# Graph attention with residual and layer norm: the row scale found at a slot's end, its sums in PSUM, the moments one slot later

## The chip, the cores and the metric

One NeuronCore of a Trainium2 chip (trn2). The metric is the device time of one launch in microseconds; the kernel before took 638.26 us (median of 3 runs, 637.56 to 639.02).

## What is computed

64 graphs of 128 nodes and 384 channels, 12 heads of 32 channels, in float32. The adjacency matrix is both spatial and edge encoding, so it enters the scores twice. A row of scores that is all zero gives zero attention.

```python
q = (x @ Wq.T); k = (x @ Wk.T); v = (x @ Wv.T + bv)          # split in 12 heads of 32
scores = einsum('bqhd,bkhd->bhqk', q, k) * 384**-0.5 + (adj + adj)[:, None]
row_nonzero = any(scores != 0, axis=-1)
p = softmax(where(row_nonzero, scores, -inf)); p = nan_to_num(p)
y = x + einsum('bhqk,bkhd->bqhd', p, v).reshape(b, n, h) @ Wo.T + bo
out = (y - mean(y)) / sqrt(var(y) + 1e-5)
```

## The kernel before

Everything is in one hand-ordered program: each engine has its own loop over slots, with semaphores between them. Slot b (b from -1 to 64) works on several graphs at once: it begins graph b+1 and ends graph b-1. Matmuls with weights are done in three terms from a high and a low part (`TERMS`), so each is 9 matmuls for 384 channels.

TensorE, slot b: `turn(b)` (48 transposes of the probabilities), `score(b+1)` (12 heads into the four banks `scores_ps`, three column blocks m of 128 each), one and a half tiles of the next group's queries or keys (`project`), `values(b+1)`, `project_out(b-1)` into `scores_ps[0]`, `attend(b)` into `scores_ps[1]`. Slots 59 and later have no `project`. `score` waits for the bias passes, `y_ready` and `att_done` of earlier slots, since those read the banks.

VectorE, slot b, in this order: `normalise(b-1)` (writes `att_n`, L626), `find_scale(b)` (L589 to L615), `bias_and_max(b+1, 0)` and `(b+1, 1)` (L558: per head adds the adjacency, multiplies by -2, and takes the row's minimum as `neg_max`; the queries carry half the scale), `attention_low(b-1)` (L630), `bias_and_max(b+1, 2)`, `keep_turned_high(b)`, `keep_first(b)`, `keep_v(b+1)`, `residual(b-1)` (y, L639, then `bn_stats` L642 and `bn_aggr` L644).

ScalarE (ACT), slot b: `attention_high(b-1)` (L503), `keep_turned_low(b)`, `softmax_top(b+1, m)` (L473: 12 exponentials with row sums, one `probs_ready` a column block), `keep_second(b)`, `normalised(b-2)` (writes `out_n`), `split_x_high`.

GpSimd (POOL), slot b: `find_rstd(b-2)` (L295 to L303: rstd and shift from the moments), `sum_scores(b+1)` (L287: halves the rows of `nscores` by additions into `tree`, in parts of `PARTS` and in `TREE` levels; a row's sum together with `neg_max` tells whether the row is all zero), `add_bias(b)` (L275), `split_x_low` (L268; in three slots of four).

`find_scale` makes of the tree's rest a sum (`total`), of that and `neg_max` a flag (`nonzero`), of the row sums a reciprocal (`recip`), and of both the row scale, transposed. The scale goes through memory (SP's DMAs to `scale_mem` and back to `scale_t`) so that it lies along the columns of the attention output, where `normalise` multiplies with it. The last graph takes the direct way: `scale_n` goes through TensorE's transposes.

Of the kernel before, what the change touches and what calls it, by code (L numbers as in the profile page):

```python
# [10 lines left out]
P = 128  # L11
NB = 64
HID = 384
HEADS = 12
D = HID // HEADS
KT = HID // P
HPT = P // D
# [8 lines left out]

TERMS = ((HI, HI), (HI, LO), (LO, HI))
FULL = KT * len(TERMS)
TREE = 3
REST = P >> TREE  # L30

PARTS = ((0, 2 * HPT), (2 * HPT, HEADS))
STEPS = TREE * len(PARTS)
XBUFS = 3

# [3 lines left out]
def build(nc, xt, xn, adj, wq, wk, wv, wo, bv, bo, out):  # L39
    with ExitStack() as ctx:  # L40
        def sb(name, shape, dt=F32):
            return ctx.enter_context(nc.sbuf_tensor(name, shape, dt))

        def ps(name, shape):
            return ctx.enter_context(nc.psum_tensor(name, shape, F32))

        def sem(name):
            return ctx.enter_context(nc.semaphore(name))
# [21 lines left out]
        neg_max = sb("neg_max", [P, 2, HEADS])  # L70
        row_sum = sb("row_sum", [P, 2, HEADS])
        tree = sb("tree", [P, 2, HEADS, P // 2])
        total = sb("total", [P, HEADS])
        nonzero = sb("nonzero", [P, HEADS])
        recip = sb("recip", [P, HEADS])
        row_scale = sb("row_scale", [P, D])
        scale_rows = sb("scale_rows", [P, 2, D])
# [19 lines left out]
        scores_ps = [ps(f"scores_ps{j}", [P, 512]) for j in range(HPT)]  # L97
# [3 lines left out]

        turn_ps = [qk_ps[0], v_ps, qk_ps[1], spare_ps]
        att_ps = scores_ps[1]


        scale_mem = nc.dram_tensor("scale_mem", (2, D, P), F32, kind="Internal").ap()
# [34 lines left out]
        total_done = sem("total_done")  # L141
        recip_done = sem("recip_done")
        nonzero_done = sem("nonzero_done")
        scale_found = sem("scale_found")
# [18 lines left out]
        def has(b):  # L163
            return 0 <= b < NB

        def wait(eng, semaphore, value):

            if value > 0:
                eng.wait_ge(semaphore, value)

        def direct(b):

            return b == NB - 1
# [4 lines left out]
        def out_bank(b):  # L178
            return scores_ps[0] if has(b + 1) else scores_ps[2]
# [11 lines left out]
        def slots_with_tiles(b):  # L191

            return min(b + 2, NB - GRP)
# [65 lines left out]
        def _(pool):  # L259
# [17 lines left out]
            def sum_scores(b):  # L277

                wait(pool, total_done, b - 1)
                for part, (low, high) in enumerate(PARTS):  # L280
                    pool.wait_ge(biased, KT * b + high // HPT)
                    src = nscores[:, b % 2, low:high]
                    for n in range(TREE):
                        width = P >> (n + 1)
                        if n:
                            pool.wait_ge(tree_step, b * STEPS + part * TREE + n)
                        nc.gpsimd.tensor_tensor(tree[:, b % 2, low:high, 0:width], src[:, :, 0:width],  # L287
# [32 lines left out]
        def _(pe):  # L320
# [23 lines left out]
            def score(b):  # L344

                g, cols = b // GRP, slice(b % GRP * P, (b % GRP + 1) * P)
                if b == 0:
                    pe.wait_ge(first_keys, KT)
                    pe.wait_ge(first_queries, KT)
                elif b % GRP == 0:  # L350
                    pe.wait_ge(kept_first, slots_with_tiles(b - 2))
                    pe.wait_ge(kept_second, slots_with_tiles(b - 2))

                wait(pe, biased, KT * b)
                wait(pe, y_ready, b - 2)
                wait(pe, att_done, b - 1)
                for m in range(KT):
                    for j in range(HPT):
                        rows = slice(j * D, (j + 1) * D)
                        last = nc.tensor.matmul(scores_ps[j][:, m * P:(m + 1) * P], q_t[rows, g % 2, m, cols],  # L360
                                                k_t[rows, g % 2, m, cols], start=True, stop=True)
                last.then_inc(scores_done, 1)
# [184 lines left out]
        def _(dve):  # L547
# [16 lines left out]
            def keep_v(b):  # L564
                dve.wait_ge(vproj_done, b + 1)
                wait(dve, pv_done, b - 1)
                nc.vector.tensor_tensor(v_n[:, b % 2], v_ps[:, 0:HID], bv_rows[:], ALU.add).then_inc(v_ready, 1)
# [17 lines left out]
            def find_scale(b):  # L585

                half = b % 2
                dve.wait_ge(tree_step, STEPS * (b + 1))
                nc.vector.reduce_sum(total[:], tree[:, half, :, 0:REST], axis=mybir.AxisListType.X).then_inc(total_done, 1)  # L589
                dve.wait_ge(total_done, b + 1)  # L590
                nc.vector.scalar_tensor_tensor(out=nonzero[:], in0=neg_max[:, half], scalar=0.0, in1=total[:],
                                               op0=ALU.not_equal, op1=ALU.max).then_inc(nonzero_done, 1)
                dve.wait_ge(probs_ready, KT * (b + 1))
                wait(dve, recip_done, b)
                nc.vector.reciprocal(recip[:], row_sum[:, half]).then_inc(recip_done, 1)
                dve.wait_ge(nonzero_done, b + 1)
                dve.wait_ge(recip_done, b + 1)
                if direct(b):

                    nc.vector.scalar_tensor_tensor(  # L600
                        out=scale_n[:].rearrange("p (h d) -> p h d", h=HEADS),
                        in0=nonzero[:].unsqueeze(2).to_broadcast([P, HEADS, D]), scalar=0.0,
                        in1=recip[:].unsqueeze(2).to_broadcast([P, HEADS, D]),
                        op0=ALU.not_equal, op1=ALU.mult).then_inc(scale_ready, 1)
                    return
                if b == 0:
                    dve.wait_ge(zeroed, 2)
                nc.vector.scalar_tensor_tensor(out=row_scale[:, 0:HEADS].rearrange("p (j m) -> p m j", m=KT),
                                               in0=nonzero[:].rearrange("p (m j) -> p m j", m=KT), scalar=0.0,
                                               in1=recip[:].rearrange("p (m j) -> p m j", m=KT),  # L610
                                               op0=ALU.not_equal, op1=ALU.mult).then_inc(scale_found, 1)
                dve.wait_ge(scale_found, b + 1)
                wait(dve, rows_out, DMA * (b - 1))

                nc.vector.transpose(scale_rows[:, half], row_scale[:]).then_inc(rows_turned, 1)  # L615
# [18 lines left out]
            def residual(b):  # L634
                half = b % 2
                dve.wait_ge(oproj_done, b + 1)
                dve.wait_ge(xb_ready, b + 1)
                wait(dve, out_ready, b - 1)
                nc.vector.tensor_tensor(y[:, half], out_bank(b)[:, 0:HID], x_n[:, b // 2 % 2, half],  # L639
                                        ALU.add).then_inc(y_ready, 1)  # L640
                dve.wait_ge(y_ready, b + 1)
                nc.vector.bn_stats(stats[:], y[:, half]).then_inc(stats_done, 1)  # L642
                dve.wait_ge(stats_done, b + 1)
                nc.vector.bn_aggr(mean_var[:, half], stats[:]).then_inc(moments_done, 1)  # L644

            def normalised_last(b):
                half = b % 2
                dve.wait_ge(rstd_ready, b + 1)
                dve.wait_ge(stored[b // 2 % 2], b // 4 * DMA)
                nc.vector.tensor_scalar(out_n[:, b // 2 % 2, half], y[:, half], mean_var[:, half, 0:1],  # L650
                                        rstd[:, half:half + 1], ALU.subtract, ALU.mult).then_inc(last_ready, 1)
# [19 lines left out]
            for b in range(-1, NB + 1):  # L671
                if has(b - 1):
                    normalise(b - 1)
                if has(b):
                    find_scale(b)
                if has(b + 1):
                    bias_and_max(b + 1, 0)
                    bias_and_max(b + 1, 1)
                if has(b - 1):
                    attention_low(b - 1)  # L680
                if has(b + 1):
                    bias_and_max(b + 1, 2)
                if has(b):
                    keep_turned_high(b)
                if projected(b):
                    keep_first(b)
                if has(b + 1):
                    keep_v(b + 1)
                    if has(b - 1):
                        residual(b - 1)  # L690
                elif b == NB:
                    residual(b - 2)
                    residual(b - 1)
            normalised_last(NB - 1)


# [33 lines left out]
```

## Time and profile before

| | before |
|---|---|
| median of 3 runs | 638.26 us (637.56 to 639.02) |
| the profiled execution | 637.14 us, its span 635.4 us |
| TensorE matmul busy | 593.0 us, 93% of the span |
| weight load, VectorE, ScalarE, GpSimd | 82%, 76%, 78%, 71% |
| TensorE clock granted | 0.993 |
| chain that ended last | PE 74%, DVE 19%, issue 3%, DMA 3% |

In the profile PE is the matmul side of TensorE, PEld its weight loads, DVE is VectorE. A group of instructions has its line, engine, operation and tiles, then busy time and mean duration. In the timelines a row is the start in us from the span's start, the duration in us, engine and line; in brackets the idle time before it and what ended it. Durations of matmuls are modelled at their end, and overlap.

### The profile page before, as it was taken

What the parts mean: (1) busy time and instruction counts of PE and PEld (TensorE: products, weight loads), DVE (VectorE), ACT (ScalarE), POOL (GpSimd) and SP (SyncE); (2) the same over time, 40 slices, a digit from 0 to 9 for tenths busy, and PEclk for the clock granted to TensorE, in tenths of its full rate; (3) what the DMA queues carried; (4) which work ended last, traced back from release to release, by engine and by line L of the source; (5) the groups of instructions that cost most, each with busy time, mean ns of one, the idle gap of its engine ahead of it and who ended that gap; (6) DMA issues with size and microseconds to landing.
All of it is one profiled execution on the core that took longest, in us unless ns stands there. A gap on an engine that the chain in (4) does not pass through costs nothing.

```text
span 635.4 us, 23731 instructions
## 1 busy us (share of the span) xinstructions
PE 593.0 (93%) x8448; PEld 518.5 (82%) x8448; DVE 482.7 (76%) x2380; ACT 497.6 (78%) x1975; POOL 452.6 (71%) x691
## 2 busy tenths in 40 slices
PE   8899999999999999999999999999999999999773
PEld 5788888888888888888888888888878888888663
DVE  4778877877877877877877877777887787787884
ACT  5688778778788778778878877877878878877882
POOL 1577777777687687778768678777768768667773
PEclk9999999999999999999999999999999999999998
DMA  8311324232142422224242132423214222112221
GB/s 305 134 37 46 109 85 137 75 110 84 47 134 87 125 84 64 95 82 135 84 126 81 39 121 86 132 80 91 91 58 135 86 75 86 52 52 86 87 79 50
DMA packets 34749, 59.63 MB, mean 94 GB/s; under 512 B 10568, under 2 KB 24008, under 8 KB 34632
## 3 DMA queue, kind: packets, MB, share of 16 engines
q1 hardware_dynamic: 34200, 57.53, 28.1%
q8 instruction: 67, 1.10, 0.7%
q10 hardware_dynamic: 432, 0.59, 0.3%
q14 instruction: 50, 0.41, 0.2%
HBM read 44.50 MB, written 13.62 MB: 91 GB/s over the span
## 4 chain that ended last, share of the span: by engine, by line
PE 74%; DVE 19%; issue 3%; DMA 3%; ACT 0%; POOLq 0%; POOL 0%; DVEq 0%
PE qk_ps L339 32%; PE scores_ps L430 16%; PE v_ps L373 15%; PE scores_ps L360 9%; DVE y L639 6%; DVE stats L642 5%; DVE att_n L626 5%; DMA scale_t<-scale_mem 2%; PE scores_ps L442 1%; DMA scale_mem<-scale_rows 1%; DMA x_raw<-xt 1%; DVE nscores L558 1%; DVE mean_var L644 0%; PE v_ps L442 0%; PE qk_ps L442 0%
## 5 line engine op out<-in xcount | busy, mean ns | idle before, releaser
L473 ACT ACTIVATE probs<-nscores,neg_max 128x128 f32<-128x128 f32 x768 | 297.5, 389 | 34.7 <-DVE neg_max L558 34.7
L287 POOL TENSOR_TENSOR tree<-nscores 128x512 f32<-128x512 f32 (+1 forms) x128 | 143.1, 1118 | 115.1 <-DVE neg_max L558 115.1
L558 DVE CUSTOM_DVE_ANT_0 nscores<-scores_ps,adj_n 128x128 f32<-128x128 f32 x768 | 171.9, 286 | 4.0 <-PE scores_ps L360 1.7
L473 ACT ACTIVATION_READ_ACCUMULATOR probs<-nscores,neg_max 128x1 f32 x768 | 144.0, 187 | 0.0
L287 POOL TENSOR_TENSOR tree<-tree 128x128 f32<-128x128 f32 (+2 forms) x256 | 127.8, 499 | 20.1
L639 DVE TENSOR_TENSOR y<-scores_ps,x_n 128x384 f32<-128x384 f32 x64 | 35.7, 558 | 110.2 <-PE scores_ps L430 110.2
L430 PE MATMUL scores_ps<-w_o,att_t 128*128 128x384 f32 x576 | 112.8, 341 | 7.1 <-DVE att_t L630 4.6
L373 PE MATMUL v_ps<-w_v,x_t 128*128 128x384 f32 x576 | 111.7, 338 | 1.1 <-ACT probs_t L498 1.1
L339 PE MATMUL qk_ps<-x_t,w_k 128*128 128x512 f32 (+1 forms) x540 | 108.9, 346 | 0.0
L373 PEld LDWEIGHTS v_ps<-w_v,x_t 128*128 128x128 f32 x576 | 102.2, 188 | 7.4 <-ACT probs_t L498 1.9
L339 PE MATMUL qk_ps<-x_t,w_q 128*128 128x512 f32 (+1 forms) x540 | 107.5, 343 | 0.0
L430 PEld LDWEIGHTS scores_ps<-w_o,att_t 128*128 128x128 f32 x576 | 99.0, 190 | 8.6 <-DVE att_t L630 8.6
L503 ACT ACTIVATE att_t<-att_n 128x384 fp32r<-128x384 f32 x64 | 33.5, 524 | 83.6 <-DVE att_n L626 83.6
L339 PEld LDWEIGHTS qk_ps<-x_t,w_k 128*128 128x128 f32 x540 | 84.9, 190 | 13.6 <-issue 0.2
L339 PEld LDWEIGHTS qk_ps<-x_t,w_q 128*128 128x128 f32 x540 | 83.9, 188 | 13.2
L360 PE MATMUL scores_ps<-k_t,q_t 32*128 32x128 f32 x1536 | 61.0, 286 | 23.6 <-DVE att_n L626 22.6
L360 PEld LDWEIGHTS scores_ps<-k_t,q_t 32*128 32x128 f32 x1536 | 50.6, 186 | 29.0 <-issue 28.9
L268 POOL TENSOR_TENSOR x_t<-x_raw,x_t 128x512 fp32r<-128x512 f32 x45 | 58.4, 1300 | 13.2 <-ACT x_t L492 13.2
L275 POOL TENSOR_TENSOR x_n<-x_n,bo_rows 128x384 f32<-128x384 f32 x64 | 64.5, 1008 | 0.0
L389 PEld LDWEIGHTS qk_ps<-ident,probs 32*128 32x128 f32 x1536 | 52.9, 137 | 14.1 <-issue 14.1
L558 DVE DVE_READ_ACCUMULATOR2_ANT neg_max<- 128x1 f32 x768 | 63.8, 83 | 0.0
L498 ACT ACTIVATE probs_t<-qk_ps 128x384 f32<-128x384 f32 (+1 forms) x128 | 62.0, 484 | 1.8 <-PE spare_ps L399 1.2
(71 smaller groups left out, 928.0 us busy)
## 6 DMA issues: line engine op xcount, KB each, us to landing
x_n<-xn SPq DMA_DIRECT2D x32, 384.0 KB, 4.8
scale_t<-scale_mem SPq DMA_DIRECT2D x63, 192.0 KB
out<-out_n SPq DMA_DIRECT2D x31, 384.0 KB, 2.6
x_raw<-xt SPq DMA_DIRECT2D x15, 768.0 KB, 5.4
adj_n<-adj SPq DMA_DIRECT2D x32, 128.0 KB, 4.4
scale_mem<-scale_rows SPq DMA_DIRECT2D x63, 16.0 KB
x_raw<-xt SPq DMA_DIRECT2D x3, 256.0 KB, 4.8
nscores<-wq ACTq DMA_DIRECT2D x3, 192.0 KB, 4.2
```

The source lines that it names most:

```text
L268: nc.gpsimd.tensor_tensor(x_t[:, g % XBUFS, LO, k], x_raw[:, g % 2, k], x_t[:, g % XBUFS, HI, k].bitcast(F32), ALU.subtract).then_inc(x_sp ...
L275: nc.gpsimd.tensor_tensor(row, row, bo_rows[:], ALU.add).then_inc(xb_ready, 1)
L287: nc.gpsimd.tensor_tensor(tree[:, b % 2, low:high, 0:width], src[:, :, 0:width], src[:, :, width:2 * width], ALU.add).then_inc(tree_step, 1)
L339: last = nc.tensor.matmul(qk_ps[n][:, start:end], w[:, a, k, cols], x_t[:, g % XBUFS, c, k, start:end], start=(k == 0 and i == 0), stop=(k ...
L360: last = nc.tensor.matmul(scores_ps[j][:, m * P:(m + 1) * P], q_t[rows, g % 2, m, cols], k_t[rows, g % 2, m, cols], start=True, stop=True)
L373: last = nc.tensor.matmul(v_ps[:, 0:HID], x_t[:, g % XBUFS, a, k, cols], w_v[:, c, k], start=(k == 0 and n == 0), stop=(k == KT - 1 and n ...
L389: last = nc.tensor.transpose(turn_ps[j][:, h * D:(h + 1) * D], probs[rows, b % 2, h], ident[rows, rows])
L430: last = nc.tensor.matmul(out_bank(b)[:, 0:HID], att_t[:, b % 2, a, k], w_o[:, c, k], start=(k == 0 and n == 0), stop=(k == KT - 1 and n = ...
L473: last = nc.scalar.activation(probs[:, b % 2, h], nscores[:, b % 2, h], ACT.Exp, bias=neg_max[:, b % 2, h:h + 1], scale=-1.0, accum_out=ro ...
L498: nc.scalar.activation(turned_rows(b, j), turned_bank(b, j), ACT.Copy).then_inc(turned_low, 1)
L558: last = nc.vector.tensor_tensor_reduce(out=nscores[:, half, h], in0=scores_ps[j][:, m * P:(m + 1) * P], in1=adj_n[:, b // 2 % 2, half], s ...
L639: nc.vector.tensor_tensor(y[:, half], out_bank(b)[:, 0:HID], x_n[:, b // 2 % 2, half], ALU.add).then_inc(y_ready, 1)
```

## The change

- The tree has 2 levels instead of 3, and 3 parts of 4 heads (one for each block m of biased scores) instead of one of 8 and one of 4: additions of 128x256 and 128x128, three times. What is left to sum on VectorE is 32 columns a head, not 16.
- `total` and `nonzero` lie in `scores_ps[3]` (PSUM), columns 0 to 23, instead of SBUF. `score(b)` therefore waits for `scale_found` too.
- `find_scale` of graph b+1 is done at the end of slot b, behind `keep_v(b+1)` and ahead of `residual(b-1)`, instead of at the start of slot b+1, behind `normalise`.
- `bn_stats` and `bn_aggr` leave `residual` for a function `moments`, which runs for graph b-2 in slot b, behind `normalise(b-1)`. In the last slots they are placed by hand.

```diff
-TREE = 3
+TREE = 2
 REST = P >> TREE
-PARTS = ((0, 2 * HPT), (2 * HPT, HEADS))
+PARTS = tuple((m * HPT, (m + 1) * HPT) for m in range(KT))
...
-        total = sb("total", [P, HEADS])
-        nonzero = sb("nonzero", [P, HEADS])
...
+        total = scores_ps[3][:, 0:HEADS]
+        nonzero = scores_ps[3][:, HEADS:2 * HEADS]
...
                 wait(pe, att_done, b - 1)
+                wait(pe, scale_found, b)
...
                 nc.vector.tensor_tensor(y[:, half], out_bank(b)[:, 0:HID], x_n[:, b // 2 % 2, half],
                                         ALU.add).then_inc(y_ready, 1)
+
+            def moments(b):
+                half = b % 2
                 dve.wait_ge(y_ready, b + 1)
                 nc.vector.bn_stats(stats[:], y[:, half]).then_inc(stats_done, 1)
...
                 if has(b - 1):
                     normalise(b - 1)
-                if has(b):
-                    find_scale(b)
+                if has(b - 2) and has(b + 1):
+                    moments(b - 2)
                 if has(b + 1):
                     bias_and_max(b + 1, 0)
                     bias_and_max(b + 1, 1)
...
                 if has(b + 1):
                     keep_v(b + 1)
+                    find_scale(b + 1)
                     if has(b - 1):
                         residual(b - 1)
-                elif b == NB:
+                elif b == NB - 1:
+                    moments(b - 2)
+                else:
                     residual(b - 2)
+                    moments(b - 2)
                     residual(b - 1)
+                    moments(b - 1)
             normalised_last(NB - 1)
```

## Rows read from the trace of the kernel before

**Rows 1.** The page, part 1: busy us of TensorE, share of the span.
```profile
PE 593.0 (93%) x8448; PEld 518.5 (82%) x8448; DVE 482.7 (76%) x2380; ACT 497.6 (78%) x1975; POOL 452.6 (71%) x691
```

**Rows 2.** The chain of waits in mid-run: start us, us, what.
```profile
300.39 0.57 DVE y L639
...
300.99 0.57 DVE stats L642
...
301.68 0.55 DVE att_n L626
...
302.36 0.95 PE scores_ps L360 x24
```

**Rows 3.** The list of waits: us in total, times, longest us.
```profile
DVE y L639 <- PE scores_ps L430: 110.2, 63, 2.6
...
PE scores_ps L360 <- DVE att_n L626: 22.6, 61, 1.0
```

**Rows 4.** Timeline of TensorE: scores of slots 1, 59 and 62; mid-run attention and transposes.
```profile
37.60 0.95 PE L360 MATMUL scores_ps<-k_t,q_t 32*128 32x128 f32 x24
...
300.29 0.86 PE L413 MATMUL scores_ps<-probs_t,v_n 128*32 128x128 f32 x24
...
301.80 0.22 PE L389 MATMUL spare_ps<-ident,probs 32*128 32x32 f32 x1
...
586.58 0.95 PE L360 MATMUL scores_ps<-k_t,q_t 32*128 32x128 f32 x24 [0.35 <-DVE att_n L626]
...
611.80 0.95 PE L360 MATMUL scores_ps<-k_t,q_t 32*128 32x128 f32 x24 [1.00 <-DVE att_n L626]
```

**Rows 5.** Timeline of TensorE in slot 0, last transpose and first scores.
```profile
28.46 0.22 PE L389 MATMUL spare_ps<-ident,probs 32*128 32x32 f32 x1
28.48 0.39 PE L360 MATMUL scores_ps<-k_t,q_t 32*128 32x128 f32 x4
```

**Rows 6.** Timeline of the last slot: attention matmuls, and what waited for them.
```profile
623.30 0.86 PE L413 MATMUL scores_ps<-probs_t,v_n 128*32 128x128 f32 x24
...
624.23 0.56 DVE L626 TENSOR_TENSOR att_n<-scores_ps,probs_t 128x384 f32<-128x384 f32 x1 [2.08 <-PE scores_ps L413]
```

**Rows 7.** Timeline of VectorE, mid-run slot.
```profile
302.13 0.34 DVE L589 TENSOR_REDUCE total<-tree 128x12 f32<-128x192 f32 x1
...
302.51 0.17 DVE L591 SCALAR_TENSOR_TENSOR nonzero<-neg_max,total 128x12 f32<-128x12 f32 x1
302.60 0.22 DVE L595 RECIPROCAL recip<-row_sum 128x12 f32<-128x12 f32 x1
...
303.38 0.29 DVE L558 CUSTOM_DVE_ANT_0 nscores<-scores_ps,adj_n 128x128 f32<-128x128 f32 x1
...
305.07 0.56 DVE L630 TENSOR_TENSOR att_t<-att_n,att_t 128x384 fp32r<-128x384 f32 x1
```

**Rows 8.** Timeline of ScalarE, same slot: the last of 12 softmax heads.
```profile
308.90 0.19 ACT L473 ACTIVATION_READ_ACCUMULATOR probs<-nscores,neg_max 128x1 f32 x1
```

**Rows 9.** Timeline of GpSimd, same slot; last row from its groups by form.
```profile
302.65 0.19 POOL L295 TENSOR_SCALAR var_eps<-mean_var 128x1 f32<-128x1 f32 x1
...
303.62 0.27 POOL L303 TENSOR_SCALAR shift<-mean_var,rstd 128x1 f32<-128x1 f32 x1
...
305.30 1.50 POOL L287 TENSOR_TENSOR tree<-nscores 128x512 f32<-128x512 f32 x1 [1.42 <-DVE neg_max L558]
...
L287 POOL TENSOR_TENSOR tree<-tree 128x128 f32<-128x128 f32 x128 | 59.5, 465 | 10.0
```

**Rows 10.** Timelines of VectorE and GpSimd where both ran.
```profile
46.55 1.28 POOL L268 TENSOR_TENSOR x_t<-x_raw,x_t 128x512 fp32r<-128x512 f32 x1
46.82 0.34 DVE L589 TENSOR_REDUCE total<-tree 128x12 f32<-128x192 f32 x1
47.20 0.66 DVE L591 SCALAR_TENSOR_TENSOR nonzero<-neg_max,total 128x12 f32<-128x12 f32 x1
...
301.30 1.27 POOL L268 TENSOR_TENSOR x_t<-x_raw,x_t 128x512 fp32r<-128x512 f32 x1
```

More of the change, by code:

```diff
@@ L588, in find_scale @@
                 dve.wait_ge(tree_step, STEPS * (b + 1))
-                nc.vector.reduce_sum(total[:], tree[:, half, :, 0:REST], axis=mybir.AxisListType.X).then_inc(total_done, 1)
+                nc.vector.reduce_sum(total, tree[:, half, :, 0:REST], axis=mybir.AxisListType.X).then_inc(total_done, 1)
                 dve.wait_ge(total_done, b + 1)
-                nc.vector.scalar_tensor_tensor(out=nonzero[:], in0=neg_max[:, half], scalar=0.0, in1=total[:],
+                nc.vector.scalar_tensor_tensor(out=nonzero, in0=neg_max[:, half], scalar=0.0, in1=total,
                                                op0=ALU.not_equal, op1=ALU.max).then_inc(nonzero_done, 1)
@@ L601, in find_scale @@
                         out=scale_n[:].rearrange("p (h d) -> p h d", h=HEADS),
-                        in0=nonzero[:].unsqueeze(2).to_broadcast([P, HEADS, D]), scalar=0.0,
+                        in0=nonzero.unsqueeze(2).to_broadcast([P, HEADS, D]), scalar=0.0,
                         in1=recip[:].unsqueeze(2).to_broadcast([P, HEADS, D]),
@@ L608, in find_scale @@
                 nc.vector.scalar_tensor_tensor(out=row_scale[:, 0:HEADS].rearrange("p (j m) -> p m j", m=KT),
-                                               in0=nonzero[:].rearrange("p (m j) -> p m j", m=KT), scalar=0.0,
+                                               in0=nonzero.rearrange("p (m j) -> p m j", m=KT), scalar=0.0,
                                                in1=recip[:].rearrange("p (m j) -> p m j", m=KT),
```

## The prediction

> **What bounds the kernel now.** I read the page first: TensorE is busy for 593.0 of 635.4 us [rows 1], so what can be won is the little time in which it waits, once a slot. The chain of waits in the middle of the run repeats one pattern: output projection, then on VectorE `y`, `stats`, the short `mean_var`, `att_n`, and then `scores_ps` on TensorE again [rows 2]. The list of waits prices it: TensorE waited 61 times for `att_n`, 22.6 us in all, while VectorE idled 110.2 us for the output projection (1.75 us a slot) [rows 3]. So VectorE has room, but its work lies badly: four instructions stand between two TensorE stages, and only `y` and `att_n` have to. The moments (0.57 us, then `mean_var`) merely lie ahead of `att_n` in the queue.
>
> All times below count from the start of a slot's scores, S (302.36 in the slot shown). Scores start at 37.60 in slot 1 and at 586.58 in slot 59 [rows 4], 58 slots, thus 9.465 us each. The attention matmuls start at 300.29 [rows 4], a period later at S+7.39.
>
> **Moments a slot later.** `bn_stats` and `bn_aggr` leave the place between `y` and `att_n`. What is late next? First `att_n` itself: it needs the attention matmuls. Where only they held it, they started at 623.30 and it at 624.23, 0.93 later [rows 6]. In the middle slot that gives 301.22 in place of 301.68 [rows 2, 4]; `y`, started at 300.39, lets its follower start 0.60 later, at 300.99, so it isn't the bound. From `att_n`'s start to the scores is 0.68 [rows 2]. Scores: S+7.39+0.93+0.68 = S+9.00. Second, TensorE's own queue: the last transposes start at 301.80 [rows 4], and in slot 0, with no such wait, scores follow them by 0.02 [rows 5]. That is 301.82, S+8.93 in the next slot: not the bound by 0.07. The gain is 0.46 a slot, more than the 0.37 that the list of waits shows, since that counts only from the transposes' modelled end.
>
> The moved moments run behind `att_n`, from 0.45 after its start (301.68 to 302.13) [rows 2, 7], thus S-0.23, and take 0.60 plus about 0.2: done at S+0.57, while VectorE would wait for the scores until S+1.02 (303.38) [rows 7]. Cost nothing; that cover is what `find_scale` leaves. Behind them: POOL's `find_rstd` (302.65 to 303.89, 1.24) [rows 9] from about S+0.65 to S+1.89, just before the first tree addition could start. Slack 0.2; ACT's `normalised` comes after the softmax, S+6.7, so it and the store behind it aren't touched.
>
> **`find_scale` from the slot's start to its end.** It leaves 1.25 us between `att_n` and the bias passes (302.13 to 303.38) [rows 7], where it lay beside the scores: little is won, at most 0.04. It now stands ahead of `y`, and everything in its queue (`y`, `att_n`, the scores) waits for what it waits for. Two loops form.
> - ACT's: the last accumulator read ends at 308.90+0.19, S+6.73 [rows 8]. 0.07 until VectorE sees it (as for the matmuls, 0.86 long of the 0.93 [rows 6]); from `recip` to the next work 0.78 (302.60 to 303.38) [rows 7]; `y` 0.61, one step of 0.60 and a little [rows 2]; 0.68. Sum S+8.87, under 9.00. `y` starts at S+7.58 instead of S+7.50, unseen behind the matmuls.
> - POOL's: see the tree.
>
> **Three sums of four heads, two levels.** POOL's first addition began at 305.30, 1.92 after the bias passes; eight passes take 1.69 of that (305.07 less 303.38) [rows 7, 9], so it follows them by 0.23. With four heads: S+1.02+0.85+0.23 = S+2.10. Four heads cost 0.75 (half of 1.50) and then 0.47 [rows 9], with 0.08 between. The third level is gone; POOL adds 1152 columns a slot instead of 1344, in six instructions as before. `attention_low` reads two SBUF operands at S+2.71 [rows 7], in the middle of the first part; the two take turns (next part), which puts the second addition off by about 0.4: first part done at S+3.74. Two parts of 1.25 more: S+6.24, the last scores having been biased long before. VectorE was free at 1.75 before `y`, S+5.75 [rows 3]. The reduction has 384 elements instead of 192: 0.34 [rows 7] becomes at least that and at most 0.57, `bn_stats` on 384 [rows 2]; I take 0.54, being nearest to `bn_stats`. With 0.04 on either side and 0.09 from flag to `recip`: `recip` at S+6.95, against S+6.80 from ACT. Then 0.78, 0.61, 0.68: S+9.02. This loop ties with the matmuls', and I take **9.02**.
>
> **Sums and flags in PSUM.** At 47.20 the flag, with both tensors in SBUF, took 0.66 instead of the 0.17 of mid-run [rows 7, 10], and ended 0.03 after POOL's 46.55 subtraction; the reduction at 46.82, one SBUF operand, took its usual 0.34 under the same subtraction, and `att_n` at 301.68, one operand in PSUM, its 0.55 under POOL's 301.30 [rows 2, 10]. So a VectorE instruction with two SBUF tensors takes turns with POOL's and others don't. At its new place the flag would meet `add_bias`, queued right behind the tree; with `total` in PSUM it has one SBUF tensor and goes through. The price is that VectorE writes to PSUM, which no row shows. Lower bound 0 (nothing is removed that a write to SBUF did); upper, nearest row: `y`, reading PSUM, takes 0.57 where `attention_low`, all SBUF, takes 0.56 [rows 2, 7], so 0.01 an instruction. I take 0, and keep 0.05 for each of three instructions, +0.15, for what a write may add.
>
> The Trainium skill ("VectorE: DVE Perf Modes", section on the TRN2 errata) speaks against the change: it charges VectorE 120 cycles for a PSUM source and 58 for an SBUF one. By that the flag and `row_scale` would cost an estimated 0.13 us more a slot, 7.5 us in all; the rows above show 0.01 for `y` and speak against it. For the turn-taking, its page "SBUF — State Buffer" (section "SBUF: two separate sides") has whichever starts first hold the shared port pair for its whole instruction; this trace agrees for the flag (0.66 for 0.17).
>
> `score` gets one wait more, for `scale_found`: `find_scale` stands ahead of a `y` that `score` already waits for. Cost 0. The DMA round trip of `scale_t` starts most of a slot sooner in relation to its use. SP's queue holds it behind the store of `out`, about S+7.6, where it becomes ready anyway; the user comes over a slot later.
>
> **The ends.** Slots without projections (scores 586.58 to 611.80: 25.2 us for three) [rows 4] are shorter than 9.02, and here the new loops decide, since no projections lie beside the softmax: 3 x 9.02 = 27.1, a loss of 1.8. After the last scores the same delay of `y` puts `att_n` and the output projection off, by something between 0 and the 0.6 that one such slot loses; I take 0.4, as `scale_n` comes sooner but `y` lies ahead of `att_n`. At the start I count nothing.
>
> **Sum.** 58 x (9.465 - 9.02) = 25.8 gained, less 2.2: 23.6 us. The profiled execution took 637.14 us (span 635.4 and 1.7 around it): 613.5. The median of the runs is 638.26, 1.1 above it: 614.6 us.
>
> **Rivals.**
> - *Held in the new place* (chance 0.27). The find-scale stretch costs 0.1 to 0.35 more than I sum. With PSUM writes at +0.13 the period is 9.15: 18.3 less 2.2, 622 us. If PSUM doesn't free the flag from POOL, it stays until `add_bias` ends, S+7.25, and `recip` starts at S+7.20 instead of 6.95: 9.27, 11.3 less 2.5, 629.5 us. For it: the POOL loop has no slack at all. Against: the unheld `att_n`.
> - *Slower* (0.07): results in PSUM come late to the next instruction. Total to flag to `row_scale` are two dependent steps of VectorE on a loop without slack; each tenth costs 5.8 us. At +0.45 together the gain is gone, beyond it the tail's 2.2 decide; at +0.6 the period is 9.62, +9.0+2.8: 650 us. Against: the short steps by which VectorE reads what TensorE wrote there.
> - *It doesn't do what it says* (0.03): `att_n` waits for the attention matmuls at 301.68 anyway and the moments were hidden; 638 us, no change. Against: the 0.93.
> - *More than forecast* (0.04): `attention_low` slips between the additions and TensorE's queue is the bound, 8.93: 31 less 2, 609 us.
> - The forecast (0.59): periods of 9.00 to 9.12, 611 to 620 us.
>
> The range takes the forecast and most of the first rival: 610.5 to 630. About 0.2% (1.3 us) is what a measurement of this kernel can tell from no change. Faster 0.90, same 0.03, slower 0.07.
>
> **What would show it.** Right: `stats` stands behind `att_n`, the wait of `scores_ps` for `att_n` falls from 0.37 to under 0.1 a slot, periods of 9.0; `y` starts 0 to 0.15 behind the output projection, held by `recip` or the tree; the flag at 0.17 while `add_bias` runs; the last slots longer than 8.7. Wrong: `att_n` behind a `y` over 0.15 late (rival one or two, told apart by the flag's length and by the distance from reduction to flag), or behind matmuls ending where they did (rival three).

## The result, and the profile after

The changed kernel takes 619.83 us (median of 4, 619.18 to 620.35), against 638.64 us before: a ratio of 0.9706, interval 0.9687 to 0.9725. Faster, as forecast, by 18.8 us where 23.6 were expected. The profiled execution took 619.18 us, span 617.3. The page of after, busy time and the chain that ended last:

```profile
span 617.3 us, 23793 instructions
...
PE 593.2 (96%) x8448; PEld 519.0 (84%) x8448; DVE 495.3 (80%) x2380; ACT 497.5 (81%) x1975; POOL 424.6 (69%) x691
...
PE 87%; DVE 3%; POOL 2%; ACT 2%; DMA 1%; issue 1%; SPq 0%; POOLq 0%; DVEq 0%; ACTq 0%
```

TensorE's busy time is that of before [rows 1]: only its waiting went. VectorE's share of the chain fell from 19% to 3%. The timelines of one mid-run slot of after, all engines, answer to [rows 4, 7, 9]:

```profile
302.41 0.56 DVE L627 TENSOR_TENSOR att_n<-scores_ps,scale_t 128x384 f32<-128x384 f32 x1 [0.27 <-PE scores_ps L414]
302.88 0.55 DVE L646 BATCH_NORM_STATS2 stats<-y 128x6 f32<-128x384 f32 x1
...
302.99 0.22 PE L390 MATMUL spare_ps<-ident,probs 32*128 32x32 f32 x1
303.22 0.95 PE L361 MATMUL scores_ps<-k_t,q_t 32*128 32x128 f32 x24
...
306.14 0.66 POOL L287 TENSOR_TENSOR tree<-tree 128x128 f32<-128x128 f32 x1
...
309.27 1.02 POOL L275 TENSOR_TENSOR x_n<-x_n,bo_rows 128x384 f32<-128x384 f32 x1
...
309.35 0.56 DVE L590 TENSOR_REDUCE scores_ps<-tree 128x12 f32<-128x384 f32 x1 [0.50 <-POOL tree L287]
309.94 0.17 DVE L592 SCALAR_TENSOR_TENSOR scores_ps<-neg_max,scores_ps 128x12 f32<-128x12 f32 x1
310.03 0.22 DVE L596 RECIPROCAL recip<-row_sum 128x12 f32<-128x12 f32 x1
...
310.71 0.56 DVE L640 TENSOR_TENSOR y<-scores_ps,x_n 128x384 f32<-128x384 f32 x1
```

`stats` stands behind `att_n`, the flag takes 0.17 while GpSimd's bias addition (309.27) runs (0.17 to 0.18 in all 64 slots), and the next scores start at 312.35: slots of 9.13 us in mid-run. The list of waits answers to [rows 3]:

```profile
DVE nscores L559 <- PE scores_ps L361: 38.0, 63, 1.4
...
DVE scores_ps L590 <- POOL tree L287: 32.8, 63, 1.1
...
PE scores_ps L361 <- DVE att_n L627: 3.3, 4, 1.0
```

The 22.6 us of `scores_ps` waiting for `att_n` are 3.3 now, and 110.2 us of VectorE idling ahead of `y` have moved to other places. Scores of slots 1, 59 and 62 in after's timeline:

```profile
38.03 0.95 PE L361 MATMUL scores_ps<-k_t,q_t 32*128 32x128 f32 x24
...
568.04 0.95 PE L361 MATMUL scores_ps<-k_t,q_t 32*128 32x128 f32 x24
...
594.14 0.95 PE L361 MATMUL scores_ps<-k_t,q_t 32*128 32x128 f32 x24 [1.01 <-DVE att_n L627]
```

With [rows 4]: 58 slots take 530.0 instead of 549.0 (-19.0; 9.138 each); the three last 26.1 instead of 25.2 (+0.9); what follows them 23.2 instead of 23.6 (-0.4); and slot 1 comes 0.4 later (the very first scores, ahead of every changed instruction, were already 0.8 late in this execution). Together -18.1, the difference of the spans.

### The profile page after: what moved, and what is told of

Same layout as the page of the kernel before. It is cut to its first block, busy times and chain, and to the rows that moved or that the text cites. A ratio compares the mean times of both kernels' runs of the same rounds, so it can differ in the third digit from the quotient of the medians.

```text
span 617.3 us, 23793 instructions
## 1 busy us (share of the span) xinstructions
PE 593.2 (96%) x8448; PEld 519.0 (84%) x8448; DVE 495.3 (80%) x2380; ACT 497.5 (81%) x1975; POOL 424.6 (69%) x691
## 4 chain that ended last, share of the span: by engine, by line
PE 87%; DVE 3%; POOL 2%; ACT 2%; DMA 1%; issue 1%; SPq 0%; POOLq 0%; DVEq 0%; ACTq 0%
PE qk_ps L339 32%; PE scores_ps L431 15%; PE v_ps L374 15%; PE scores_ps L361 10%; PE scores_ps L414 7%; PE qk_ps L390 7%; POOL tree L287 2%; ACT probs L474 1%; DMA scale_mem<-scale_rows 1%; DVE nscores L559 1%; PE spare_ps L390 1%; DMA scale_t<-scale_mem 1%; DVE att_n L627 1%; PE v_ps L390 0%; DVE y L640 0%
## 5 line engine op out<-in xcount | busy, mean ns | idle before, releaser
L474 ACT ACTIVATE probs<-nscores,neg_max 128x128 f32<-128x128 f32 x768 | 297.5, 389 | 37.5 <-DVE neg_max L559 37.5
L287 POOL TENSOR_TENSOR tree<-nscores 128x256 f32<-128x256 f32 x192 | 143.9, 749 | 31.4 <-DVE neg_max L559 31.4
L287 POOL TENSOR_TENSOR tree<-tree 128x128 f32<-128x128 f32 x192 | 101.3, 528 | 15.0
L590 DVE TENSOR_REDUCE scores_ps<-tree 128x12 f32<-128x384 f32 x64 | 35.9, 561 | 32.8 <-POOL tree L287 32.8
L390 PE MATMUL qk_ps<-ident,probs 32*128 32x32 f32 x1536 | 59.9, 223 | 1.0 <-issue 1.0
```

What stands on the lines that cost most here:

```text
L390: last = nc.tensor.transpose(turn_ps[j][:, h * D:(h + 1) * D], probs[rows, b % 2, h], ident[rows, rows])
L474: last = nc.scalar.activation(probs[:, b % 2, h], nscores[:, b % 2, h], ACT.Exp, bias=neg_max[:, b % 2, h:h + 1], scale=-1.0, accum_out=ro ...
```

## The experiments

The question: why 9.13 a slot and not 9.02, and which part of the change carries the gain? The time from `att_n`'s start to the first score matmul, the step below, is 0.81 (302.41 to 303.22); before it was 0.68 [rows 2].

**Wait moved.**

```diff
+                wait(pe, scale_found, b)
                 wait(pe, y_ready, b - 2)
                 wait(pe, att_done, b - 1)
-                wait(pe, scale_found, b)
```

> The changed kernel with one line moved: score waits for scale_found before it waits for att_done, not after. Theory 'wait': the slot is 9.12 us and not 9.00 since one more wait stands between att_done and the first score (att_n's start to scores 0.81 us, before 0.68). Then moving it out of that place gives the 0.13 back: slots of 9.00, about 7.5 us less than the changed kernel, 612 us. Rival 'array': scores can't start before the transposes have left TensorE (0.22 after the last one's start, where 303.22 lies); then nothing changes, 619.8 us, and att_n to scores stays 0.81.

614.39 us, ratio to before 0.9630 (0.9611 to 0.9648), 5.4 us under the changed kernel. The rival 'array' falls. Its timeline:

```profile
308.80 0.56 DVE L627 TENSOR_TENSOR att_n<-scores_ps,scale_t 128x384 f32<-128x384 f32 x1 [0.26 <-PE scores_ps L414]
...
309.50 0.95 PE L361 MATMUL scores_ps<-k_t,q_t 32*128 32x128 f32 x24
```

The step is 0.70, and slots take 9.03.

**One wait.** From graph 3 on `score` waits for `att_done` alone. VectorE gives the other three signals ahead of that one, so they are implied.

```diff
-                wait(pe, biased, KT * b)
-                wait(pe, y_ready, b - 2)
+                if b < 3:
+                    wait(pe, biased, KT * b)
+                    wait(pe, scale_found, b)
                 wait(pe, att_done, b - 1)
-                wait(pe, scale_found, b)
```

> The changed kernel whose score waits for att_done alone from graph 3 on (it implies the other three, since VectorE reaches it after them). Theory 'wait': at least as much as with the wait moved, att_n to scores at most 0.68, slots of 9.00 or, where TensorE's queue is next, 8.93: 609 to 612 us. Rival 'array': no change, 619.8 us, scores still 0.22 behind the last transpose's start.

612.22 us, 0.9591 (0.9570 to 0.9612). The step in its timeline is 0.63.

```profile
424.73 0.56 DVE L627 TENSOR_TENSOR att_n<-scores_ps,scale_t 128x384 f32<-128x384 f32 x1 [0.27 <-PE scores_ps L414]
...
425.36 0.93 PE L361 MATMUL scores_ps<-k_t,q_t 32*128 32x128 f32 x24
```

**Other waits behind.** All four waits kept, `att_done` written first.

```diff
+                wait(pe, att_done, b - 1)
                 wait(pe, biased, KT * b)
                 wait(pe, y_ready, b - 2)
-                wait(pe, att_done, b - 1)
                 wait(pe, scale_found, b)
```

> The changed kernel with att_done waited for first and the three others (biased, y_ready, scale_found, all long met) behind it. Theory 'wait': each wait behind the one that ends last costs again, so att_n's start to scores grows from 0.81 to 0.9 or more, slots of 9.2 to 9.35: 625 to 633 us. Rival: only the number of waits counts, not their place: 0.81 and 619.8 us as in the changed kernel.

611.21 us, 0.9575 (0.9550 to 0.9600): neither. As I had worded it, theory 'wait' falls: with three waits written behind the last to end the kernel is as fast as with one (the intervals overlap). Its timeline has a step of 0.63, and 0.77 in the slot after it:

```profile
409.52 0.56 DVE L627 TENSOR_TENSOR att_n<-scores_ps,scale_t 128x384 f32<-128x384 f32 x1 [0.27 <-PE scores_ps L414]
...
410.15 0.93 PE L361 MATMUL scores_ps<-k_t,q_t 32*128 32x128 f32 x24
...
418.49 0.56 DVE L627 TENSOR_TENSOR att_n<-scores_ps,scale_t 128x384 f32<-128x384 f32 x1 [0.26 <-PE scores_ps L414]
...
419.26 0.95 PE L361 MATMUL scores_ps<-k_t,q_t 32*128 32x128 f32 x24
```

The built programs resolve it: the build puts the waits in another order than the source, one on the first matmul, the others in wait instructions of their own, of up to two each. What stands between the transposes and the first matmul in three slots of four, each bracket one wait instruction, and the step in the traces:

```
kernel            wait instructions, in their order        on the matmul   att_n to scores
before            (att_done, y_ready)                      biased          0.68
changed           (att_done) (scale_found, y_ready)        biased          0.81
wait moved        (y_ready) (att_done, scale_found)        biased          0.70
one wait          none                                     att_done        0.63
waits behind      (y_ready) (scale_found, biased)          att_done        0.63
```

Ordered by how many wait instructions are left when `att_done` arrives, its own counted: 0, 1, 1, 2 give 0.63, 0.68, 0.70, 0.81. Every fourth slot tests this once more. Its graph is the first of a group, `score` also waits for `kept_first` and `kept_second`, and the build groups the waits anew: one is left with one wait, two with the waits behind, and the steps there are 0.70 and 0.77. In the three others the number left is the same as in their other slots, and so is the step. Wait instructions that come ahead of the last signal to arrive cost nothing: two of them in the kernel with the waits behind give the 0.63 of none. From there on the first adds 0.05 to 0.07 us and the second 0.07 to 0.13.

The 0.63 isn't the signal's alone. In those slots the scores start 0.05 behind the last transpose, at the pace of the transposes themselves, so TensorE's queue lets them start no sooner; where `att_n` came late, and in the three last slots, the step is 0.60 to 0.61. That the fourth wait makes a second wait instruction, behind `att_done`'s arrival, is the 0.12 a slot by which I was off.

**Implied waits out elsewhere too.** The kernel with one wait, and `attend` without `v_ready` and `biased`, `turn` without `kept_first`, `project_out` without `y_ready`.

```diff
-                pe.wait_ge(v_ready, b + 1)
-                free_scores(b + 1)
+                if b == 0:
+                    pe.wait_ge(v_ready, b + 1)
+                    free_scores(b + 1)
...
-                pe.wait_ge(kept_first, slots_with_tiles(b - 1))
+                if b < 2:
+                    pe.wait_ge(kept_first, slots_with_tiles(b - 1))
```

> The kernel whose score waits for att_done alone, with the implied waits taken out of the other two places too: attend waits for the turned rows only, turn no more for kept_first, project_out no more for y_ready. Theory 'wait': a wait costs about 0.1 where it comes behind the one that ends last, and about nothing elsewhere; in these places all are long met, and TensorE's loads pause 0.25 and 0.20 there. If that pause is the waits', the period shrinks by up to 0.1 to 0.3 (594 to 606 us); rival 'the array empties' before the other kind of matmul: the pauses stay and the time is 612.

611.87 us, 0.9595 (0.9579 to 0.9611), as with one wait (612.22). The pauses of the weight loads in its list of waits are unchanged (15.6 and 14.5 us with one wait):

```profile
PEld scores_ps L416 <- issue: 15.8, 63, 0.4
PEld qk_ps L391 <- issue: 14.5, 64, 1.5
```

In the built program one wait instruction is left ahead of each, where there were two, and the pauses stay. So the waits taken out had no part in them, which fits the rule: nothing arrives late there. What the pauses are, the rival's emptying array or something else, was not tested.

**Sums in SBUF, without the wait.** `total` and `nonzero` in SBUF tensors again, no wait for `scale_found`.

> The changed kernel with total and nonzero back in SBUF, and so without the wait for scale_found. Theory: the flag meets GpSimd's bias addition and is held until 0.03 after it, about 0.4 in place of 0.17 us; y comes about 0.2 later, and att_n, which waits 0.27 for the attention matmuls, doesn't notice. So PSUM buys nothing and its wait costs: with theory 'wait' 612 us, with 'array' 619.8. Rival 'PSUM carries it': the held flag puts the scores off by 0.1 to 0.3 a slot, 626 to 637 us.

616.86 us, 0.9658 (0.9637 to 0.9679). Flag, attention matmuls and `y` in its timeline:

```profile
316.54 0.39 DVE L591 SCALAR_TENSOR_TENSOR nonzero<-neg_max,total 128x12 f32<-128x12 f32 x1
...
317.24 0.86 PE L413 MATMUL scores_ps<-probs_t,v_n 128*32 128x128 f32 x24
...
317.52 0.53 DVE L639 TENSOR_TENSOR y<-scores_ps,x_n 128x384 f32<-128x384 f32 x1
...
318.17 0.56 DVE L626 TENSOR_TENSOR att_n<-scores_ps,scale_t 128x384 f32<-128x384 f32 x1
```

The flag is held, 0.39 for 0.17, but `att_n` comes 0.93 behind the attention matmuls, as in the changed kernel, and 0.65 behind `y`, where 0.45 is enough in a run below: covered, with 0.2 to spare. The waits are built as before the change, and the step is 0.70. That is why this is faster than the changed kernel, whose step of 0.81 costs more than the held flag. The kernel with the wait moved has the step of 0.70 too, and its sums in PSUM: 614.39 us, 2.5 less.

**The same with one wait**, which parts the held flag from the wait instruction.

> The kernel whose score waits for att_done alone, with total and nonzero in SBUF. Theory: the flag is held until the bias addition ends (0.39 for 0.17), y comes 0.15 to 0.2 later and att_n hardly, since it waits 0.26 for the attention matmuls; slots of 8.98 to 9.03. In the three slots without projections nothing covers it, 0.2 each. Sum 0.6 to 3 us over the one with PSUM (612.2): 613 to 615. Rival 'PSUM carries it': 620 us or more.

614.58 us, 0.9617 (0.9593 to 0.9641): 2.4 us above the same kernel with PSUM (612.22, on another chip), and 3.4 above the one with the waits behind (611.21, on the same chip). The flag takes 0.38 on average, from its groups by line:

```profile
L592 DVE SCALAR_TENSOR_TENSOR nonzero<-neg_max,total 128x12 f32<-128x12 f32 x64 | 24.3, 379 | 2.2
```

So PSUM seems worth 2 to 3 us where its wait is placed well, and loses where it isn't. All three pairs say so, but in each the intervals overlap. The traces place only 0.6 us of it: the three slots without projections take 26.1 for 25.5 (and 26.3 for 25.8 in the other pair), about the 0.2 each that I had expected.

**The moments alone.** The kernel before, with `moments(b - 2)` behind `normalise(b - 1)` and ahead of `find_scale(b)`; nothing else.

```diff
                     normalise(b - 1)
+                if has(b - 2) and has(b + 1):
+                    moments(b - 2)
                 if has(b):
                     find_scale(b)
```

> The kernel before with the moments alone moved behind the next att_n; find_scale, tree and SBUF as before. Theory: the whole gain is in this move. The bias passes start 0.8 later (S+1.8), the softmax ends at S+7.5, ahead of the transposes at S+8.2: slots of 9.00 with theory 'wait' (three waits as before), 9.12 with 'array'; the last slots as before: 611 to 620 us. Rival 'both needed': without find_scale out of the way the bias passes' 0.8 shows, slots of 9.4 or more, 636 us or slower.

634.10 us, 0.9935 (0.9913 to 0.9957), 4 us of the 18.8: my theory falls, and nearly so does its rival. Its list of waits names what I hadn't priced:

```profile
DVE att_n L626 <- DMA scale_t<-scale_mem: 31.9, 43, 2.0
...
PE scores_ps L360 <- DVE att_n L626: 13.0, 29, 1.1
```

**Its scale not waited for.** To take that wait away, `normalise` multiplies by `bv_rows`, which has long been there; `find_scale` and its DMAs still run, and SP's queue waits for each trip instead. The scaling of the attention is left out.

```diff
-                    dve.wait_ge(scale_in[b % 2], DMA * (b // 2 + 1))
-                    scale = scale_t[:, b % 2]
+                    scale = bv_rows[:]
```

> The run with the moments alone moved, but normalise multiplies with bv_rows, which has long been there, and doesn't wait for the scale; find_scale and its way through memory still run. The attention's scaling is so left out. Theory 'round trip': the 31.9 us for which att_n waited for scale_t were what the move lost; slots of 9.03 throughout, 610 to 614 us. Rival 'bias passes 0.8 late': 630 us or more.

621.15 us, 0.9721 (0.9694 to 0.9747). 13 us of the loss were the wait for the scale's way through memory. Some 9 us are left above the kernel with one wait, to which both theories were blind in part; 2.5 of them lie in the three slots without projections (28.0 for 25.5). Its timeline and list of waits, in a slot in which GpSimd subtracts:

```profile
403.18 1.29 POOL L271 TENSOR_TENSOR x_t<-x_raw,x_t 128x512 fp32r<-128x512 f32 x1
...
403.72 0.77 DVE L594 SCALAR_TENSOR_TENSOR nonzero<-neg_max,total 128x12 f32<-128x12 f32 x1
...
410.28 0.86 PE L416 MATMUL scores_ps<-probs_t,v_n 128*32 128x128 f32 x24
...
411.26 0.21 PE L392 MATMUL qk_ps<-ident,probs 32*128 32x32 f32 x1
...
ACT probs L476 <- DVE neg_max L561: 92.9, 64, 3.7
...
PEld qk_ps L392 <- issue: 20.8, 64, 1.5
```

The flag is held 0.6 by the subtraction, the bias passes follow, the softmax waits 92.9 us for them (37.5 after the change), and the next transposes, which start about 0.8 behind the attention matmuls elsewhere, start at 411.26, 0.98 behind them (410.28).

**`find_scale` ahead of the moments**, still at the slot's start.

> As the run with the moments alone moved, but find_scale stands ahead of the moments at the slot's start, so that the scale sets out 0.6 us sooner on its way through memory. Theory 'round trip': the move alone gains 0.45 a slot only where the scale is back in time; with the moments ahead of find_scale it was back about 7.0 after the transpose, 0.4 too late in most slots. Now it is in time, slots of 9.02, last slots as before: 611 to 614 us. Rival 'VectorE's bias passes': the passes, still 0.8 late, are what costs, and the time stays at 634.

645.16 us, 1.0123 (1.0090 to 1.0155): slower than before, against my theory. Setting out earlier, `find_scale` meets the subtraction with `row_scale`, of two SBUF tensors as well:

```profile
318.48 1.28 POOL L268 TENSOR_TENSOR x_t<-x_raw,x_t 128x512 fp32r<-128x512 f32 x1
...
318.85 0.95 DVE L608 SCALAR_TENSOR_TENSOR row_scale<-nonzero,recip 128x12 f32<-128x12 f32 x1
...
DVE att_n L626 <- DMA scale_t<-scale_mem: 27.8, 28, 2.6
```

The hold puts off both the scale and the bias passes.

**The same, its scale not waited for** (the scaling of the attention left out as above).

> The same for the run with find_scale ahead of the moments: the scaling of the attention is left out. There row_scale and the flag, both of two SBUF tensors, are held by GpSimd's subtraction (0.46 us on average each, for 0.18). If the loss went only through the late scale_t (27.8 us), 617 us; if it went through the late bias passes and the softmax to the transposes, 635 us or more. I expect some of both, 625 to 635.

639.46 us, 1.0009 (0.9994 to 1.0025), above the 625 to 635 that I expected. 5.7 us went through the scale (7.3 by the ratios). The larger part is left: 18.3 us above the run before last, from which this one differs by the order of `find_scale` and the moments alone. Between the two `row_scale` goes from 0.19 to 0.69 on average, and the softmax's wait for the bias passes from 92.9 to 115.7 us. That the one leads to the other and so to the time is argued, not shown link by link.

**`find_scale` alone.** The changed kernel with the moments back in `residual`.

```diff
                     normalise(b - 1)
-                if has(b - 2) and has(b + 1):
-                    moments(b - 2)
...
                         residual(b - 1)
+                        moments(b - 1)
```

> The changed kernel with the moments back between y and the next att_n: find_scale at the slot's end, tree and PSUM as changed. Theory: the stretch from y to att_n is again 1.29 and the wait behind att_done is there (0.81), so scores at S+7.54+1.29+0.81, slots of 9.64: 648 us, slower than the kernel before by 10. Rival 'the move of find_scale gains by itself', since VectorE is free earlier for the bias passes: 638 us or less.

652.01 us, 1.0217 (1.0200 to 1.0234). The stretch from `y` to the scores in its timeline, 2.08, and in the chain before 1.97 [rows 2]:

```profile
313.17 0.56 DVE L640 TENSOR_TENSOR y<-scores_ps,x_n 128x384 f32<-128x384 f32 x1
313.77 0.56 DVE L646 BATCH_NORM_STATS2 stats<-y 128x6 f32<-128x384 f32 x1
...
314.46 0.54 DVE L627 TENSOR_TENSOR att_n<-scores_ps,scale_t 128x384 f32<-128x384 f32 x1
...
315.25 0.95 PE L361 MATMUL scores_ps<-k_t,q_t 32*128 32x128 f32 x24 [0.45 <-DVE att_n L627]
```

Slots of 9.57 (9.64 expected) and last slots of up to 10.2. The moments by themselves give 4 us, the rest of the change by itself costs 14; together they give 18.8.

**The tree of before** (`TREE = 3`, eight heads and four) in the changed kernel.

> The changed kernel with the tree of before (eight heads, then four, three levels) in front of find_scale at the slot's end. Theory: the tree ends at S+7.5 instead of S+6.2, the reduction (0.34 again) and all behind it stand in front of y: y at S+8.75, scores at S+10.2, about 678 us. Rival 'the tree is covered': under 625 us.

670.40 us, 1.0509 (1.0485 to 1.0533), slots of 9.88. VectorE waits for the tree ahead of `y`:

```profile
313.85 0.36 DVE L590 TENSOR_REDUCE scores_ps<-tree 128x12 f32<-128x192 f32 x1 [1.85 <-POOL tree L287]
...
315.00 0.53 DVE L640 TENSOR_TENSOR y<-scores_ps,x_n 128x384 f32<-128x384 f32 x1
...
315.45 0.55 DVE L627 TENSOR_TENSOR att_n<-scores_ps,scale_t 128x384 f32<-128x384 f32 x1
```

Without the new tree, the rest of the change loses 32.6 us.

Not tried: sums in PSUM with `find_scale` at the slot's start. The scores write `scores_ps[3]` just then, and the other banks are in use by TensorE as well; at the slot's end that bank is free, which is one more reason for the place.

## Why the prediction came out as it did

- **`att_n` 0.93 behind the attention matmuls: right.** 301.48 to 302.41 in after; the moments behind it were covered (VectorE then waited 0.58 for the scores).
- **"`score` gets one wait more ... Cost 0": wrong, and the main miss.** The term "from `att_n`'s start to the scores is 0.68" became 0.81, so S+7.39+0.93+0.68 = S+9.00 became S+9.13. I asked what the wait waits for (nothing) and not where its instruction stands. It costs 5.4 us against the kernel with the same four waits and this one written ahead. With `att_done` on the matmul itself it is 7.6 to 8.6 us, but that also saves what the kernel before paid.
- **TensorE's queue at 0.02 behind the last transpose: right, but after's profile hides it.** There the scores start 0.23 behind it (302.99 to 303.22), at its modelled end, so that the list of waits shows 3.3 us and the chain of waits is TensorE throughout. With one wait and with `att_done` first the scores start 0.05 behind it (425.31 to 425.36 in the timeline with one wait). A matmul's modelled end isn't the time from which the next could start. Slots there take 8.94 to 9.06 for the most part, near the 8.93 that I had named for this bound.
- **The tree's loop: oversized.** `recip` came at S+6.81, not 6.95: the second addition was put off by 0.2 (0.66 for 0.47), not 0.4. From `recip` to `y` it took 0.68, not 0.78, and from `y` to an `att_n` that doesn't read it 0.45 (315.00 to 315.45 with the old tree), not 0.61, which I had taken from `stats`, which reads `y`. So it doesn't tie with the matmuls' loop. With these terms `att_n` could start at S+7.94, and it started at S+8.31, behind the matmuls. The working has a slip as well: its own figures (2.10+0.75+0.08+0.47+0.4) make the first part end at S+3.80, not S+3.74; it ended at S+3.58. So 9.02 was taken from a loop that doesn't bind, and that it lay near the matmuls' 9.00 is luck.
- **PSUM: right in size** (flag 0.17, reduction 0.56 for the 0.54 taken, `row_scale` 0.18). From reduction to flag it takes 0.59 with the sums in PSUM (309.35 to 309.94) and 0.59 in SBUF (315.95 to 316.54): results in PSUM don't come late, and the rival 'slower' falls. The Trainium skill's cycle table ("VectorE: DVE Perf Modes", section on the TRN2 errata) would add an estimated 0.13 us a slot; the trace doesn't show it. The held flag of the first rival came true in SBUF, 0.39 for 0.17, but behind the matmuls' cover it costs some 2 to 3 us and not 11.
- **`find_scale`'s move: priced on the wrong side.** I called the earlier start of the scale's DMAs a thing that costs nothing, and the move a cost. Moved alone, the moments push the scale's first DMA from 1.69 to 2.38 behind `att_n`, and a trip that had been back in time is late 43 times: 13 us. A cover that is used up isn't seen in the trace of before, where `att_n` waited 2.4 us in all for the scale.
- **The ends.** Last slots +0.9 (1.8 forecast), what follows them -0.4 (+0.4): the shorter steps behind `y`, and `scale_n` in time.

Taken together: the sum was off by 5.2 us, 619.83 for 614.6, some quarter of the gain. The 58 slots came out 6.8 us longer than forecast; the ends, 1.7 better, and the start, 0.4 worse, hide part of that, which is luck too.

## What to carry to other kernels

Ask of each edit to a saturated loop what every moved instruction pushes by its own length, DMAs first: the moments' move, to which my arithmetic gave the whole gain, gives 4 us without the rest of the change, which seemed only to cost. Where several semaphores guard one instruction, let the one that arrives last sit on the instruction itself, or else in the last wait ahead of it (here 0.07 us dearer), leave out those that it implies, and look at the built program for where they ended up. Here that is worth 1.3% more: the changed kernel with `att_done` first takes 611.21 us, 0.9575 of before.

## What the runs showed of the hardware

- Wait instructions on TensorE's queue cost time from the last semaphore to arrive on, also those that are met: the step from `att_n` to the scores is 0.60 to 0.63 with none left, 0.68 to 0.71 with one, 0.77 to 0.82 with two. Ahead of it they cost nothing (0.63 with two, 0.63 with none).
- VectorE instructions with two SBUF tensors waited for GpSimd's tensor operation to end, also tiny ones of 12 columns: a flag of 0.17 took 0.39 and 0.77, a `row_scale` of 0.18 took 0.95. With one of the two in PSUM the flag didn't wait (0.17 under a bias addition). The Trainium skill too has a VectorE operation with two SBUF inputs take turns with GpSimd's ("SBUF — State Buffer", section "SBUF: two separate sides").
- Results that VectorE wrote to PSUM cost it about what they cost to SBUF: 0.56 and 0.55 for the reduction of 384, and 0.59 in both from its start to that of the flag, which reads them.
